# Two layers of cross-attention and feed-forward on one core: values projected one batch ahead, weights loaded in portions, three thin products stacked into one

## What is computed

```python
# x [16,100,256], ctx [16,361,256], mask [16,1,100,361] (layer 0 only)
x = x + tanh(g_xattn[0]) * attn0(ln(x), ctx, ctx, mask)   # 16 heads of 16, biases on q, k, v, o
x = x + tanh(g_ffn[0])   * moe(ln(x))                     # 8 experts of 192, top 2, and a shared one
x = x + tanh(g_xattn[1]) * attn1(ln(x), ctx)              # 16 heads of 16, no mask
x = x + tanh(g_ffn[1])   * lora_ffn(ln(x))                # 256 -> 1024 -> 256

def lora_ffn(x):                  # R = 4, E = 8
    top1 = argmax(softmax(x @ gate_W.T + gate_b))
    base = x @ wi_W.T + wi_b                       # 1024 wide
    for i in range(E):
        lora  = (x @ lora_A[i].T) @ lora_B[i].T    # 256 -> 4 -> 1024
        out_i = relu(base + lora) @ wo_W.T + wo_b
        out  += (top1 == i) * out_i
```

## Time and profile before

| | |
|---|---|
| median of 3 runs | 1007.25 us (1003.84 to 1009.66) |
| profiled execution | 1007.15 us, its span 1005.4 us |
| mean granted clock of TensorE | 0.965 |
| busy share: PE, DVE, ACT, POOL | 90%, 57%, 48%, 21% |

### The profile page before, as it was taken

The page is one execution under the profiler, slowest core; times in us unless marked ns, Lnnn a source line. Parts: engine busy times, 40 slices in busy tenths (PEclk is TensorE's granted clock), DMA queues, the critical chain, the costliest instruction groups (busy, mean ns, idle before and its releaser), DMA issues.

```text
span 1005.4 us, 24139 instructions
## 1 busy us (share of the span) xinstructions
PE 901.4 (90%) x8340; PEld 698.9 (70%) x8340; DVE 575.6 (57%) x1610; ACT 482.2 (48%) x948; POOL 211.7 (21%) x186
## 2 busy tenths in 40 slices
PE   4779999999979879999999867999999998889996
PEld 2447767676756569999999635676767666567775
DVE  5286776767756674534355445767676767543222
ACT  2345655556535564333233434656556564524442
POOL 5353212121112024242435324010101011000000
PEclk8899999999989989999999979999999999879999
DMA  6986768767677310102030596777767673000001
GB/s 178 208 197 130 146 126 152 137 130 147 123 167 163 122 58 10 67 1 66 0 96 1 165 241 146 158 141 144 143 137 154 127 144 59 1 1 8 9 16 33
DMA packets 133140, 106.94 MB, mean 106 GB/s; under 512 B 64534, under 2 KB 126630, under 8 KB 133070
## 3 DMA queue, kind: packets, MB, share of 16 engines
q1 hardware_dynamic: 129110, 102.57, 47.8%
q10 hardware_dynamic: 3968, 3.55, 1.2%
HBM read 76.56 MB, written 29.29 MB: 105 GB/s over the span
## 4 chain that ended last, share of the span: by engine, by line
PE 66%; DVE 15%; issue 7%; DMA 5%; ACT 3%; POOL 2%; SPq 1%; DVEq 0%; ACTq 0%; POOLq 0%
PE ps L1326 34%; PE ps L1417 7%; PE ps L1391 6%; PE ps L1450 6%; DVE mx L1080 4%; PE ps L1440 3%; DMA cT<-in_ctxT 3%; PE ps L1474 3%; PE ps L1436 2%; DVE ps L1076 2%; DMA x_sb<-in_x 1%; DVE onv L1100 1%; PE ps L1467 1%; DVE cTl L1053 1%; PE ps L1365 1%
## 5 line engine op out<-in xcount | busy, mean ns | idle before, releaser
L712 ACT ACTIVATE prob<-ps 128x400 f32<-128x400 f32 (+1 forms) x384 | 186.5, 504 | 109.3 <-PE ps L1440 98.1
L1076 DVE CUSTOM_DVE_ANT_0 ps<-ps,biasq 100x361 f32<-100x361 f32 x256 | 135.1, 545 | 75.6 <-PE ps L1417 70.7
L1417 PE MATMUL ps<-KS,QS 96*100 96x361 bf16 x512 | 164.5, 336 | 10.8 <-DVE mx L1076 5.1
L1080 DVE TENSOR_REDUCE mx<-ps 100x1 f32<-100x361 f32 x256 | 127.0, 529 | 71.6 <-PE ps L1417 71.0
L1440 PEld LDWEIGHTS ps<-QS,KS 98*128 98x128 bf16 x1536 | 107.1, 99 | 46.9 <-issue 11.8
L1440 PE MATMUL ps<-QS,KS 98*128 98x100 bf16 x1536 | 133.6, 209 | 3.3 <-ACT prob L712 2.2
L1391 PE MATMUL ps<-cT,wk 128*128 128x361 f32 x256 | 102.9, 515 | 28.7 <-DMA cT<-in_ctxT 18.8
L1230 DVE TENSOR_TENSOR hlo<-hh,hhi 128x400 fp32r<-128x400 f32 x88 | 51.3, 583 | 80.7 <-ACT hhi L922 76.5
L1417 PEld LDWEIGHTS ps<-KS,QS 96*100 96x100 bf16 x512 | 64.0, 125 | 46.0 <-DVE mx L1080 15.2
L515 POOL TENSOR_TENSOR kp<-kr,kp 128x722 bf16<-128x722 f32 x32 | 47.2, 1474 | 220.0 <-ACT kp L683 220.0
L1450 PE MATMUL ps<-prob,V 128*17 128x100 f32 (+1 forms) x3072 | 92.3, 254 | 0.0
(11 more groups left out here) (164 smaller groups left out, 1821.3 us busy)
## 6 DMA issues: line engine op xcount, KB each, us to landing
scr_k<-kp SPq DMA_DIRECT2D x96, 180.5 KB, 5.1
KS<-scr_k SPq DMA_DIRECT2D x64, 270.8 KB, 3.7
cT<-in_ctxT SPq DMA_DIRECT2D x32, 361.0 KB, 4.7
KS<-scr_k SPq DMA_DIRECT2D x64, 180.5 KB, 4.1
scr_q<-qp SPq DMA_DIRECT2D x48, 200.0 KB, 4.5
QS<-scr_q SPq DMA_DIRECT2D x64, 150.0 KB, 4.2
wbc<-scr_w SPq DMA_DIRECT2D x16, 400.0 KB
KS<-scr_k SPq DMA_DIRECT2D x64, 90.2 KB, 4.3
```

The lines of the kernel that those rows point to most:

```text
L712: nc.scalar.activation(prob[0:KROWS[t], t, hg, :], ps[0:KROWS[t], c % 2, 0:HQ * S], ACT.Exp).then_inc(a["exp"], 1)
L1076: nc.vector.tensor_tensor_reduce(ps[0:S, banks[h % len(banks)], 0:S2], ps[0:S, banks[h % len(banks)], 0:S2], biasq[p][:, :], 1.0, -3.0e38, ...
L1080: nc.vector.reduce_max(mx[:, h:h + 1], ps[0:S, banks[h % len(banks)], 0:S2], axis=AX.X).then_inc(a["max"], 1)
L1417: mm(ps[0:S, banks[h % len(banks)], 0:S2], QS[p][0:SROWS, h, :], KS[p][0:SROWS, h * S2:(h + 1) * S2], start=True, stop=True).then_inc(a["s ...
```

## The change

1. **Order of projections.** `values` now makes the values of batch b+1 (before: b+2), right after the first and second group of transposed scores; the first and the last step differ (no values in the first of each layer; the last but one has them). `project_k` still makes the keys of b+3, but stands around the last part of the last group, with `weigh` 1 ahead of it and `weigh` 2 and 3 behind it. The rest of the keys' way moves into the following step: `k_second`, `k3` and `k_store` now handle batch b+2. SP issues the mask and the key store ahead of the context load and of the key loads.
2. **Weights of the first feed-forward.** At the end of each of the six turns of layer 0's loop over pairs of steps SP issues the gate and up weights of one expert and a sixth of all down weights. The last two experts, the router and the shared expert follow behind step 12.
3. **Stacked products.** `BTs` holds the low-rank weight as (high, high, low) in 96 rows and `rTs` the input as (high, low, high), so that one product of 96 rows takes the place of three of 32. `choose` writes each value three times, the weight is loaded three times, and `rm` shares a place with buffers of earlier stages.

```diff
-                        project_v(l, b + 2, u, t, k, b + 3 if has_k else None)
+                        project_v(l, b + 1, 1 - u, t, k, b + 2 if has_2 else None)
...
                     if t < 2:
                         next_score(2 + t)
+                values(0)
                 if has_o:
                     turn_on(l, b - 1)
                 for t in range(NKT):
                     next_score(4 + t)
                     score_T(l, b, u, 1, t)
+                values(1)
                 next_score(7)
+                values(2)
...
-                for k in range(KT):
-                    if has_k:
-                        project_k(l, b + 3, 1 - u, i + 1 + u, 0, (k,))
-                    next_score(13 + k)
+                next_score(13)
                 score_T(l, b, u, 3, 0)
+                next_score(14)
+                weigh(l, b, u, 1)
                 next_score(15)
+                score_T(l, b, u, 3, 1)
                 if has_k:
-                    project_k(l, b + 3, 1 - u, i + 1 + u, 1)
-                score_T(l, b, u, 3, 1)
-                if has_b:
-                    turn_max(l, b + 1, b, 7)
-                weigh(l, b, u, 1)
-                score_T(l, b, u, 3, 2)
+                    project_k(l, b + 3, 1 - u, i + 1 + u, 0)
                 if not has_b:
                     norm(2 * l + 1, 2)
                     logits(l, 1)
-                values(0)
+                if has_b:
+                    turn_max(l, b + 1, b, 7)
+                score_T(l, b, u, 3, 2)
+                if has_k:
+                    project_k(l, b + 3, 1 - u, i + 1 + u, 1)
                 weigh(l, b, u, 2)
-                values(1)
                 weigh(l, b, u, 3)
-                values(2)
...
(SP)
+                if l == 0 and has_ctx:
+                    mask_load(b + 3, 1 - u, False)
+                if has_k:
+                    k_store(l, b + 2, u, i + 1)
                 if has_ctx:
                     ctx_load(l, b + 3, 1 - u, False)
...
-                if has_ctx:
-                    k_store(l, b + 3, 1 - u, i + 1 + u)
...
+                    if l == 0:
+                        expert_weights(i)
+                        expert_down(i)
                 for b in range(B - 4, B - 2):
+                    step(l, b, b % 2, b // 2 + l * IB, b + 3 < B, True)
                     if l == 0 and b == B - 4:
-                        ffn0_weights(0)
-                    step(l, b, b % 2, b // 2 + l * IB, b + 3 < B, True)
+                        for e in range(B // 2 - 2, E):
+                            expert_weights(e)
+                        shared_weights()
...
(ACT)
-                if has_b:
-                    v_copy(l, b + 1, 1 - u, 0)
                 exps(l, b, 0, (0,))
-                if has_b:
-                    v_copy(l, b + 1, 1 - u, 1)
+                if has_o and has_2:
+                    k_second(l, b + 2)
                 exps(l, b, 0, (1, 2))
                 if has_o:
                     copy_on(l, b - 1)
                 exps(l, b, 1, range(NKT))
-                if has_2:
-                    ctx_high(l, b + 2, u, i + 1)
+                if has_o and has_b:
+                    for part in range(2):
+                        v_copy(l, b + 1, 1 - u, part)
...
-            act.dma_start(BT[:, :], io["loraBT"]).then_inc(s_wf[1], 16)
+            for r in range(LPROD):
+                act.dma_start(BT[r * LR:(r + 1) * LR, :], io["loraBT"]).then_inc(s_wf[1], 16)
...
(PE)
-                split_mm(ps[:, i % 2, 0:GT], (BTh[:, cols], BTl[:, cols]), (rTh[:, tok], rTl[:, tok]),
-                         False, True).then_inc(s1["h_ready"], 1)
+                mm(ps[:, i % 2, 0:GT], BTs[:, cols], rTs[:, tok], start=False, stop=True).then_inc(s1["h_ready"], 1)
```

More of the change, by code:

```diff
@@ L34 @@
 E1, R1, F1 = 8, 4, 1024
+LR = E1 * R1
+LPROD = 3
+LROWS = LPROD * LR
 NFT1 = F1 // P
@@ L48 @@
 KLOADS = len(KRUNS) + 1
+NDLOADS = B // 2 - 2
+NDTILES = E * F // P // NDLOADS
+NDROWS = NDTILES * P
+NWG = 2 + E
+NWF0 = 3 + E + NDLOADS
 SROWS = NST * HD
@@ L562, in attn, with step @@
                     add_bias(l, g)
-                with pool.Fori(0, B // 2 - 2) as i:
-                    for u in range(2):
-                        n = 2 * i + u + 2
-                        if l == 0:
-                            bias(n, u, i + 1, False)
-                            biasT_(n, u, False)
-                        k3(l, n + 1)
-                for n in range(B - 2, B):
-                    if l == 0:
-                        bias(n, n % 2, n // 2, False)
-                        biasT_(n, n % 2, False)
-                    if n + 1 < B:
-                        k3(l, n + 1)
+                if l == 0:
+                    bias(2, 0, 1, False)
+                def step(b, u, i, has_k, has_m, has_t):
+                    if has_k:
+                        k3(l, b + 2)
+                    if l == 0 and has_m:
+                        bias(b + 3, 1 - u, i + 1 + u, False)
+                    if l == 0 and has_t:
+                        biasT_(b + 2, u, False)
+                step(0, 0, 0, False, True, True)
+                step(1, 1, 0, True, True, True)
+                with pool.Fori(1, B // 2 - 2) as i:
+                    for u in range(2):
+                        step(2 * i + u, u, i, True, True, True)
+                for b in range(B - 4, B - 2):
+                    step(b, b % 2, b // 2, True, b + 3 < B, True)
                 for g in range(GE):
@@ L800, in attn @@
                 q_second(l, 3)
+                for part in range(2):
+                    v_copy(l, 1, 1, part)
                 step(l, 0, 0, l * IB, False, True, True, True)
@@ L819, in attn @@
                 if l == 0:
-                    act.wait_ge(s_wf[0], 16 * 6)
+                    act.wait_ge(s_wf[0], 16 * NWF0)
                     high(s0, Wuh[:, 0, :], Wu[:, 0, :])
@@ L1191, in attn @@
                 for j, (wh, w, wl) in enumerate(EARLY[l]):
-                    low((s0, s1)[l], j + 1, wl, w, wh)
+                    r = slice(2 * LR, LROWS) if l == 1 and j == 1 else slice(0, P)
+                    low((s0, s1)[l], j + 1, wl, w[r], wh[r])
                 stats_end(2 * l + 1, GE * GB, B - 1)
@@ L1717, in turn_lora @@
                 for b in range(g0 * GB, g1 * GB):
-                    x = nc.tensor.transpose(ps[0:E1 * R1, 4 + b // GB, (b % GB) * S:(b % GB + 1) * S], rm[:, b, :], ident[0:S, 0:S])
+                    x = nc.tensor.transpose(ps[0:LROWS, 4 + b // GB, (b % GB) * S:(b % GB + 1) * S],
+                                            rm[:, b, :], ident[0:S, 0:S])
                 x.then_inc(s1["rT"], 1)
```

78 lines of the change are left out of this document (38 added, 40 removed).

## The result

The changed kernel took 1013.1 us (median of 20 runs, 1005.3 to 1021.2) against 1006.8 before (20 runs, 1003.8 to 1009.8): a ratio of 1.0051, with a 95% interval from 1.0030 to 1.0071. It is slower by half a per cent; 964 was forecast. (The ratio is estimated from all undisturbed runs and is not the quotient of the two medians; one of the 20 runs, the one of 1021.2, was in the slower state that some executions fall into, and is left out of it.) The other 19 scatter over 12 us, those of before over 6. The profiled execution's span is 1010.5 us.

What follows compares the result with a forecast made beforehand. TensorE, busy 90% of the span, was taken as the bound. Terms of -7.7, -24.3, -12.0, +0.1 and +0.7 summed to -43.2 us, from 1007.15 to 964.0, range 952 to 982.

Steps and rivals of the forecast that it cites:

- part 4: Waits the new order adds in each step, for keys, context, maxima and bias: 0 together, up to 1 us a step.
- Part 1: Weight loads in portions: layer 0's thirteenth step loses its 7.7 us excess, the portions cost 0; -7.7 us.
- Part 2: Stacked products in the last stage: one of 96 rows for three of 32 in each tile; -24.3 us.
- rival A: Last stage: the row change costs at 96 rows as at 32, -12 in place of -24.3; 976 us, chance 0.17.
- Part 3: An ordinary step under the new order: 17.08 us in layer 0, 15.95 in layer 1; -7.0 and -5.0 us.
- the hole: TensorE's idle time in each step until VectorE has divided the last batch's output: 0.71 us, to be removed.
- Part 5: Ends, the first and last steps of each layer: gains and losses together +0.1 us.
- The +0.7 for two more copies of a weight: Start of layer 1: 256 KB more to load at 359 GB/s, where TensorE waits for a DMA anyway; +0.7 us.
- B: Keys or context come late by half to one microsecond in most steps, 16 us in all; 980 us, chance 0.17.
- C: The reload loop of the keys becomes the bound, about 19 us a step; slower, 1042 us, chance 0.04.
- D: Hole only moves to ScalarE's copy, portions bring stalls, only the stacked products' -24 is left; 983 us, chance 0.04.
- The signs named: The prediction is wrong if the last stage shortens by less than 20 us, or the steps by nothing.

Runs made afterwards that it cites:

- gated kernel: The changed kernel with one wait more: SP issues the key load's second half only after the maxima's transfer has landed; 978.3 us, ratio 0.9730.
- `stack`: The kernel before with the stacked products alone; 987.2 us, ratio 0.9816.
- the experiment with the heads: The gated kernel with TensorE's heads 13, 14 and 15 of the next batch each one piece later; 978.2 us.

## Why the prediction was wrong

**The step that failed is in part 4, the maxima.** It took their way from TensorE's transpose to their use as 3.76 + 0.4 = 4.2 us, found 4.4 us there, and put 0 in the sum. The room was about right: from the turn to the first use 4.1 us pass in layer 1 of the gated kernel and 4.5 in layer 0, with no wait. The way was wrong. The 3.76 came from the first step of layer 1, where the transfer itself had taken 3.1; it takes 1.9 in the other steps of before, and over 4 in the new order, so that the way is 5.3 us long (in the step from 702.39, use at 707.71). The transfer of 6 KB was priced as if it flew alone.

Two moves brought it beside the key load. The new order puts the turn of the maxima directly ahead of the last group of transposed scores, and that group releases the second half of the key load; before, a weighing stood between them. So the key load now goes out 0.54 us behind the turn in place of 1.28. And ScalarE copies a part of the keys before it sends the maxima, which go out 0.92 behind the turn in place of 0.56. Together the 0.72 us of lead become 0.38 behind. The rows of the order ahead of the prediction show the first move, and I read them only for TensorE. The gate, which keeps the two apart, gave 0.66 us a step back in layer 0 and 1.42 in layer 1 ahead of the transposed scores, and with the knock-on (an interval of 21.0 us in layer 0 whose mean granted clock was 0.92, one of 19.0 in layer 1 at 0.91, the last steps of each layer) 12.9 us in layer 0 and 21.3 in layer 1. Of the keys and the context I had asked what other traffic they would meet, of the smallest transfer not.

- **Part 1, -7.7.** Too large: 0 alone and 4 beside the stacked products in the old order, 1.7 in the new one, which is not told from nothing. The new order alone had no long thirteenth step any more (18.56 us), with the large load still in one piece. I counted for the portions what the order takes away by itself. The place of the last portion, ahead of the last key store, was named in the text and priced at nothing: in the gated kernels the last interval of layer 0 was 18.0 to 22.3 us with it and 16.1 to 16.4 without.
- **Part 2, -24.3.** Measured -20.0 alone (-21.1 in the trace). The mechanism held in its numbers: 0.18 us for 96 rows, no loss at the change of rows, a tile every 2.37 us in place of 3.13, so 0.76; +0.8 for the multiplications. The size was off at the start of the stage. Two of the early tiles (4.87 and 3.44 us apart before, 4.87 and 3.40 after) wait for other things than TensorE. And the turns of the chosen rows, 96 columns wide for 32, were priced at nothing: from the first of them to the first low-rank product it was 2.39 us before and 3.42 after (3.00 in `stack`). The rule of the Trainium skill weighed there (TensorEngine Tiling (Array Packing), Key Properties) agrees with these rows, and rival A falls.
- **Part 3, -7.0 and -5.0.** By the distances from start to start in ten middle steps, gated kernel against before: the hole gave 0.67 us in layer 0 and 0.65 in layer 1, as forecast, and the small waits ahead of the values 0.42 and 0.64, for 0.2 and 0.36. ScalarE's copy cost 0.54 for the 0.39 taken (0.37 of it shows as a wait), the weighing 0.12. The heads of the next batch and the turn of their maxima cost 0.74 in layer 0, where I had taken 0, and 0.47 in layer 1, where I had taken 0.14: VectorE sets the pace of the last maxima, and the experiment with the heads showed it for most of the cost in layer 0 and nearly half of it in layer 1. So layer 0's step is 17.77 us, no shorter than before, against 17.08. Layer 1's is 15.97, against 15.95: a hit that is partly luck, since its terms missed in both directions.
- **Part 5, +0.1.** The first interval of layer 0 grew by 2.1 us (16.04 to 18.11), and not by 0.2. TensorE waits there 1.86 us for the context, and not for keys: the mask load and the key store now stand ahead of the context load in SP's queue, which is issued at 75.41 us for 70.72 before. The first interval of layer 1 was to lose 2.1 and lost 0.2 (17.04 to 16.84), and the step before last of layer 0 (17.28, forecast 16.4) takes 17.30 in the gated kernel. The +0.7 for two more copies of a weight was not measured by itself.
- **Rivals.** B had the kind of delay, a transfer that comes late in most steps, but the wrong transfer and half the price (16 us against the 34 that the gate gave back): in the loop the keys were there in time and the context too; it was the smallest transfer of the step that came late. C did not happen: with the gate the loop over the keys held a step of 15.97 us. Of D's two halves the first is true in part: of the hole of 0.67 us, 0.54 moved to ScalarE's copy.
- **The signs named.** The last stage shortened by 21.1 us, as asked; the steps did not shorten at all, by which the prediction called itself wrong.

## What to carry to other kernels

A small transfer on the path can cost more than its own time: here 4 us in place of 1.9, with a large load issued at the same moment. Where an order is moved, look at which large DMA is released by the same event, and hold that one back by a wait if it has time to spare; here this wait was worth 35 us. When a stall is taken away by one part of a change, ask whether another part has removed it already before both are counted. And where the sum of busy time falls while the span grows, go to the chain of waits first: here a line with 9% for a transfer of 6 KB led to the cause. A hit in a sum is not a hit in its terms: lay the distances between the starts of matmuls side by side, kind by kind, before a forecast step is called right.

## What the runs showed of the hardware

The lead that a transfer of 6 KB needs over a load of 0.7 MB from another engine's queue lies, in this kernel, between 0.15 and 0.42 us: with 0.42 it lands after 1.92 us, with 0.15 or less after about 4 (3.4 to 5.0 in single steps).

The traces' records of DMA packets show where the time goes. Of the transfer's 32 packets of 200 bytes the first starts 1.27 us after the issue in the kernel before, all have passed 0.23 us later, and the last count of the semaphore comes 0.40 us behind them (medians of twelve steps of layer 1). In the changed kernel the three stretches are 2.70, 0.50 and 1.04 us. So of 2.4 us more, 1.4 pass before the first packet and 0.6 behind the last one, and the packets themselves are a small part. In layer 0 it is 0.65 ahead of the first packet and 0.96 behind the last.

The Trainium skill (DMA: Bandwidth & Descriptors, Queues, rings and completion order) has each DMA engine take turns, packet by packet, between the queues that have work. By that rule alone a small transfer should get in soon; no run here shows it pass, and turns between queues say nothing of the stretch behind the last packet. What holds the transfer back in either place was not tried, only when it is held back.
